# Composing units of the last pass taken into the expert blocks, and first coefficients ahead of units

## The reference, cut to what matters

```python
h = h + _L0_attn_ref(_layernorm(h), ...)   # a state-space scan, 16 states, 256 channels
h = h + _L0_ffn_ref(_layernorm(h), ...)    # top 2 of 8 experts, each 256 -> 1024 -> 256, gated
h = h + _L1_attn_ref(_layernorm(h), ...)   # a gated recurrence
h = h + _L1_ffn_ref(_layernorm(h), ...)    # W1, W2 composed: see below
...

def _compose_weight(logits, A, B):
    vals, idx = jax.lax.top_k(logits, TOP_K)          # 32 of 64
    w = jax.nn.softmax(vals / TEMPERATURE)
    return jnp.einsum('k,kir,kro->io', w, A[idx], B[idx])
W1 = _compose_weight(fc1_logits, fc1_A, fc1_B)        # 256 x 1024
W2 = _compose_weight(fc2_logits, fc2_A, fc2_B)        # 1024 x 256
```

## Time and profile before

| what | value |
|---|---|
| time, median of 3 | 1849.72 us (1848.54 to 1851.34) |
| profiled execution | 1853.17 us, span 1851.4 us |
| PE, DVE, ACT, POOL busy | 91%, 43%, 27%, 23% |
| granted TensorE clock, mean | 0.929 |
| DMA | 129.17 MB, mean 70 GB/s |

### The profile page before, as it was taken

How to read it: one execution, slowest core, us unless ns; L and a number is a source line. 1 busy time by engine, 2 the same in 40 slices (tenths; PEclk the granted TensorE clock), 3 DMA queues, 4 the chain that set the end, 5 groups by cost and what they waited for, 6 DMA issues and landing times.

```text
span 1851.4 us, 22690 instructions
## 1 busy us (share of the span) xinstructions
PE 1680.1 (91%) x8028; PEld 1167.6 (63%) x8028; DVE 798.7 (43%) x1698; ACT 498.6 (27%) x962; POOL 418.0 (23%) x430
## 2 busy tenths in 40 slices
PE   5877499988999999999949999999899989998999
PEld 4532134437999999999935555776864456667444
DVE  3531499987111111111126760122456555675455
ACT  1234344541212221212116323123110035543000
POOL 0363577771111111211121000000100012232000
PEclk8989799997899999999989979999579999998999
DMA  5233434434344344404161000010000010000000
GB/s 168 66 94 95 110 106 96 101 71 150 146 160 175 150 160 159 162 28 160 33 182 39 1 1 28 1 46 1 1 1 0 1 46 1 1 1 1 12 17 20
DMA packets 59046, 129.17 MB, mean 70 GB/s; under 512 B 10563, under 2 KB 39268, under 8 KB 52388
## 3 DMA queue, kind: packets, MB, share of 16 engines
q1 hardware_dynamic: 54996, 116.96, 19.8%
q0 software_dynamic: 3936, 10.75, 1.7%
HBM read 196.35 MB, written 9.97 MB: 111 GB/s over the span
## 4 chain that ended last, share of the span: by engine, by line
PE 75%; DVE 10%; SPq 5%; issue 4%; POOL 3%; ACT 2%; DMA 1%; DVEq 0%; ACTq 0%; POOLq 0%
PE psum L727 39%; PE psum L1030 13%; PE psum L759 7%; PE psum L822 4%; SPq L627 3%; DVE work L1734 3%; PE psum L737 2%; PE psum L1009 2%; PE psum L938 2%; DVE work L1868 1%; SPq L624 1%; DVE work L1867 1%; POOL xn L1937 1%; ACT work L1130 1%; PE psum L1039 1%
## 5 line engine op out<-in xcount | busy, mean ns | idle before, releaser
L727 PE MATMUL psum<-work 128*128 128x128 f32 (+3 forms) x3400 | 470.4, 300 | 16.1 <-DMA work<-in_xp 15.9
L727 PEld LDWEIGHTS psum<-work 128*128 128x128 f32 x3400 | 440.0, 193 | 33.5 <-DMA work<-in_xp 15.9
L1030 PE MATMUL psum<-w_late,xn 128*128 128x512 f32 x544 | 242.0, 603 | 0.0
L1801 DVE TENSOR_TENSOR work<-sq,psum 128x512 f32<-128x512 f32 x82 | 56.3, 687 | 387.3 <-PE psum L727 387.3
L1030 PEld LDWEIGHTS psum<-w_late,xn 128*128 128x128 f32 x544 | 103.5, 193 | 128.6 <-issue 119.2
L822 PE MATMUL psum<-work,xn 128*128 128x408 f32 (+1 forms) x320 | 152.9, 591 | 31.9 <-POOL work L1959 31.4
L1734 DVE TENSOR_TENSOR_SCAN work<-psum,work 128x414 f32<-128x414 f32 (+1 forms) x160 | 158.8, 1058 | 43.2 <-POOL work L1959 38.9
L1959 POOL TENSOR_TENSOR work<-work 128x408 f32<-128x408 f32 (+1 forms) x160 | 160.9, 1039 | 58.0 <-PE psum L822 29.6
L1918 POOL TENSOR_TENSOR rs<-rs,power 128x4 f32<-128x4 f32 (+3 forms) x40 | 44.6, 1115 | 547.2 <-DVE rs L1428 540.9
L1618 DVE SCALAR_TENSOR_TENSOR h<-psum,gate,h 128x256 f32<-128x256 f32 x272 | 119.4, 480 | 106.8 <-PE psum L1030 104.1
L1130 ACT ACTIVATE work<-psum 68x364 f32<-68x364 f32 (+10 forms) x256 | 108.0, 463 | 139.5 <-PE psum L727 57.5
(11 more groups left out here) (266 smaller groups left out, 2052.9 us busy)
## 6 DMA issues: line engine op xcount, KB each, us to landing
work<-in_W SPq DMA_DIRECT2D x123, 1024.0 KB
work<-c_rows SPq DMA_DIRECT2D x48, 204.0 KB, 3.1
w_attn<-in_B SPq DMA_DIRECT2D x64, 128.0 KB, 2.4
work<-c_rows SPq DMA_DIRECT2D x32, 238.0 KB, 3.2
w_attn<-in_A SPq DMA_DIRECT2D x64, 64.0 KB, 2.2
w_attn<-in_A SPq DMA_DIRECT2D x32, 128.0 KB, 2.5
work<-in_A SPq DMA_DIRECT2D x32, 128.0 KB, 2.5
work<-y_rows SPq DMA_DIRECT2D x8, 512.0 KB, 7.8
```

What stands on the lines that cost most here:

```text
L727: mm = pe.matmul(dst, lhs(k), rhs(k), start=(k == 0), stop=(k == parts - 1))
L1030: mm = pe.matmul(dst.rearrange("p (e n) -> p e n", e=2), xn[:, k, i * P:(i + 1) * P], w_last[:, 2 * q:2 * q + 2, k, :], start=(k == 0), st ...
L1801: dve.tensor_tensor(hm[:, j % 2, 4 * q:4 * q + 4, :].rearrange("p k n -> p (k n)"), sa[:, i % 2], A.at(("e3", j, q)), ALU.mult).then_inc(s ...
```

## The change

The last pass gets 16 places of its own: eleven over `xtok` and five over `xn`, which no expert block uses. SP issues one of its units in each of the blocks 4 to 19, behind that block's weight loads, and once waits that the x rows are stored out of `xtok`. ScalarE scales one in each of the blocks 24 to 39. All sixteen report on one semaphore, waited for as a whole. The gathered y go to `ytok`, over `w13` and the start of `w2`, since `xtok` is taken. PE's order is unchanged. In the scan, the rows of steps 0 to 3 are loaded first, and units 32 to 37 follow the rows of steps 4 to 9, one each.

```diff
@@ places
-        late_slots = [work[:, (1 - r // 5) * 2 * HALVES * HIDDEN + r % 5 * (PHALF + D):][:, 0:PHALF + D] for r in range(LATE_SLOTS)]
...
+        ytok = work[:, 0:SLOTS * TILES * D].rearrange("p (s i n) -> p s i n", s=SLOTS, i=TILES)
+        xtok_flat = xtok.rearrange("p s i n -> p (s i n)")
+        xn_flat = xn[:].rearrange("p k t -> p (k t)")
+        late_slots = [xtok_flat[:, r * (PHALF + D):(r + 1) * (PHALF + D)] for r in range(XTOK_SLOTS)]
+        late_slots += [xn_flat[:, r * (PHALF + D):(r + 1) * (PHALF + D)] for r in range(PAIRS - XTOK_SLOTS)]
...
+            return sem("slot0"), 64 * (BRIDGE // PSLOTS + PAIRS)
@@ SP, load_unit
-                if i >= BRIDGE:
-                    if i in (BRIDGE, BRIDGE + 5):
-                        sp.wait_ge(sem("e3_done"), 2 * (BLOCKS if i > BRIDGE else BLOCKS - 1))
-                    if i >= BRIDGE + LATE_SLOTS:
-                        sp.wait_ge(sem("tile_used"), i - LATE_SLOTS + 1)
-                elif i >= PSLOTS:
+                if PSLOTS <= i < BRIDGE:
                     sp.wait_ge(sem("tile_used"), i - PSLOTS + 1)
@@ SP, scan
-            for i in range(PSLOTS):
-                load_unit(EARLY + i)
             for k in range(CHUNKS * N_STATE):
                 load_c(k)
+                if CRING <= k < CRING + PSLOTS:
+                    load_unit(EARLY + k - CRING)
@@ SP, blocks
+                if j == 3:
+                    sp.wait_ge(sem("x_stored"), 16 * len(GROUPS))
+                if 4 <= j < 4 + PAIRS:
+                    load_unit(BRIDGE + j - 4)
-            for i in range(BRIDGE, BRIDGE + LATE_SLOTS):
-                load_unit(i)
...
-                    sp.dma_start(xtok[:, k, t0:t1, :], y_rows[k * TOKENS:(k + 1) * TOKENS].rearrange(
+                    sp.dma_start(ytok[:, k, t0:t1, :], y_rows[k * TOKENS:(k + 1) * TOKENS].rearrange(
...
-            for i in range(BRIDGE + LATE_SLOTS, PASSES * PAIRS):
-                load_unit(i)
@@ ScalarE
-            for i in range(5):
-                scale_unit(BRIDGE + i)
+                if 8 + PAIRS <= j < 8 + 2 * PAIRS:
+                    scale_unit(BRIDGE + j - 8 - PAIRS)
             keep_y(BLOCKS - 1)
-            for i in range(5, LATE_SLOTS):
-                scale_unit(BRIDGE + i)
...
-            left = list(range(BRIDGE + LATE_SLOTS, PASSES * PAIRS))
             for d in range(DUOS):
-                if d < len(left):
-                    scale_unit(left[d])
                 ln(L1A, [d])
```

More of the change, by code:

```diff
@@ L52 @@
 BRIDGE = 3 * PAIRS
-LATE_SLOTS = 10
+XTOK_SLOTS = 11
 RING = 3
@@ L268, in build, with unit_loaded @@
         in_block = work[:, at0[0]:at0[0] + SLOTS * TILES * 2 * BLOCKS].rearrange("p (i a j) -> p i a j", a=2, j=BLOCKS)
+        ytok = work[:, 0:SLOTS * TILES * D].rearrange("p (s i n) -> p s i n", s=SLOTS, i=TILES)
[3 more added lines that the diff above has]
+        late_slots += [xn_flat[:, r * (PHALF + D):(r + 1) * (PHALF + D)] for r in range(PAIRS - XTOK_SLOTS)]
+        unit_long = lambda i: tile_long[i % PSLOTS] if i < BRIDGE else late_slots[i - BRIDGE][:, 0:PHALF]
+        unit_short = lambda i: tile_short[i % PSLOTS] if i < BRIDGE else late_slots[i - BRIDGE][:, PHALF:]
+        def unit_loaded(i):
+            if i < BRIDGE:
+                return sem(f"slot{i % PSLOTS}"), 64 * (i // PSLOTS + 1)
+            return sem("slot0"), 64 * (BRIDGE // PSLOTS + PAIRS)
         xblk = take(XR * D).rearrange("p (r n) -> p r n", r=XR)
@@ L1806, in _ @@
                 dve.wait_ge(sem("y_summed"), d + 1)
-                dve.tensor_tensor(flat(h, d), flat(h, d), flat(xtok[:, 0], d), ALU.add).then_inc(h_ready, 1)
+                dve.tensor_tensor(flat(h, d), flat(h, d), flat(ytok[:, 0], d), ALU.add).then_inc(h_ready, 1)
                 stats(L1A, d)
@@ L1988, in sum_y @@
                 pool.wait_ge(sem(f"gathered{d // 2}"), 16 * SLOTS)
-                pool.tensor_tensor(flat(xtok[:, 0], d), flat(xtok[:, 0], d), flat(xtok[:, 1], d), ALU.add).then_inc(
+                pool.tensor_tensor(flat(ytok[:, 0], d), flat(ytok[:, 0], d), flat(ytok[:, 1], d), ALU.add).then_inc(
                     sem("y_summed"), 1)
```

## The result

The changed kernel takes 1818.5 us (1817.7 to 1819.0), the kernel before beside it 1850.5; the ratio is 0.982 (95% interval 0.980 to 0.984). That is 32 us less, forecast were 34.2 (1815.5), with a range of 1808 to 1824; the time is 3.0 us above the forecast and inside the range. The profiled executions differ by 34.2 us in their span (1851.4 and 1817.2). The total is near, but its two terms are not: the tail (from the end of the last expert block to layer 1) gave 26.7 us where 24.0 were forecast, and the scan 5.8, seen at the first expert block, where 10.2 were.

The account below looks back on a forecast made before the run. After the last expert block, SP's pace of writing DMAs was taken to bound the kernel; second came the scan's start. Tail 24.0 plus scan 10.2 gave 34.2 us, from 1849.7 to 1815.5; range 1808 to 1824.

Parts of the forecast that it names:

- (a): Start of the tail: last y's scatter lands 4.4 us after issue, so the gather starts 21.3 us earlier, at 933.1.
- (b): Tail, gather to next stage: VectorE's 26 us moves 21.3 us earlier as a block; PE's last transposes end at 970.7.
- (c): Tail's end: ScalarE, no longer late by scales, lets PE start in1 at 972.5, not 996.5; tail gain 24.0 us.
- (d): Expert blocks: the moved loads and scales of 16 units cost 0, with 0 to +3 us.
- Rival D: Expert blocks: units ahead of the next expert's weights in SP's queue stall blocks; 1875 at 3.75 us each; chance 0.04.
- E: Expert blocks: the units' landing waits or the moved scales hold ScalarE; 1839.5 at worst; chance 0.04.
- C: Tail: scatter lands late, or PE at half clock sets the end; gain 18 instead of 24, 1821.5; chance 0.14.
- B: Scan: the new order gives nothing, step 10 ends where it did; 1826; chance 0.06.
- part 2: Scan: coefficients ahead of units start GpSimd 16.6 us earlier, SP's pace takes back 6.4; gain 10.2 us.
- Rival A: Scan: the new order keeps its whole gain of 16.6 us; 1809; chance 0.10.

Follow-up runs that it names:

- units ahead of the weights: The changed kernel with each unit of the last pass asked for ahead of its block's w13 load on SP; 1815.7 us, ratio 0.982.
- late scales: The changed kernel with the last pass's unit loads still early, but their 16 scales back in ScalarE's old places; 1815.4 us, ratio 0.982.
- part 1 alone: The changed kernel with the scan's old order, units 32 to 37 ahead of the first coefficients; 1823.7 us, ratio 0.986.
- part 2 alone: The kernel before with only the scan's new order of coefficients and units 32 to 37, tail as before; 1844.4 us, ratio 0.9975.

## Why the prediction was right, and where it was not

**The tail's start, (a).** The mechanism is as forecast, the size of one term was not. The scatter was taken to land 4.4 us after its issue; SP's first gather DMA is at 925.63, 2.46 us after 923.17, below even the low end of the earlier trace rows, 2.6, where its median, 4.4, was taken. From the last block to the gather it is 3.32 us, forecast 5.0, before 26.3: 1.7 us of the miss. By the 2.0 us and bytes over 436 GB/s of the Trainium skill (DMA: Bandwidth & Descriptors, Anatomy of one DMA) an estimate for this scatter of 128 KB is 2.3 us. With 2.46 us the trace agrees, and the long delay that the same section warns of for writes to HBM did not show.

**From the gather to in1, (b) and (c).** Forecast 39.4 us, measured 925.63 to 964.03, 38.4. The first sum came 5.62 us after the first gather DMA (6.04 before); this gave 0.4 us. VectorE's block is the same to 0.02 us. From its last normalising (956.96) to in1's second product it was 7.07 us, forecast 7.65: the other 0.6. Most of this is the step from ScalarE's last copy to TensorE, for which the sum had 0.4 us (972.1 to 972.5) and the trace has 0.04. The pause of TensorE was 1.5 us, not 3, which changed nothing in the sum. So the tail gives 68.4 - 41.7 = 26.7 us, not 24.0.

**The blocks, (d).** Free, as said: 443.29 against 443.28 us from the first block to the join. The run with units ahead of the weights shows that the slack is real, and how large in the tightest block: 4.2 us of delay of each w13 load bring one wait, of 0.20 us. Rival D, which needed 2.1 us in each of 16 blocks, is out; with the late scales, E is too. C is out by the landing and by the clock, which was at its full 2.4 GHz level (granted 1.00) from 940 to 952 us; B by step 10.

**The scan.** The mechanism is as forecast: SP's writing takes back a part of the gain. Mis-sized were the price per step and the landing, and the sum passed the whole gain at step 10 on to the first block. SP was taken at 4.15 us for a row and a unit: it is 4.38 to 4.79, 4.48 in the mean (SP's timeline: rows at 197.58, 201.96, 206.36, 210.75, 215.18 and 219.97). A row written right behind a unit takes 0.58 us of SP where one by itself takes 0.32, in the kernel before too (203.92 and 210.2); the prediction had 0.40 for it. Landing and start on GpSimd was 4.16 us for row 10 (219.97 to 224.13), not 3.9. So step 10 ended at 226.3, not 224.6: 8.5 us gained and not 10.2. The waits began at step 7, with 1.82 us; the prediction's working holds GpSimd from step 7 on, its list of signs names only steps 8, 9 and 10.

Of these 8.5, 5.8 arrived at the first block in this profile. From the end of step 10 to the first block the kernel before took 250.0 us and the changed one 252.7. TensorE's first four groups of out0 alone took 15.0 and 17.5 us of it, by the granted clock: 2.5 of the 2.7. This stretch has the same products in all these kernels, and its length follows the execution: 250.0, 251.2 and 250.8 us with the old order (before twice, part 1 alone), 252.7, 250.7, 250.5, 246.5 and 246.2 with the new one (changed kernel twice, units ahead of the weights, part 2 alone, late scales). In the two of 246 us the four groups took 12.7 and 12.8 us. So a single profile can't say whether part 2 gives 5 or 10 us.

Two figures stand for what part 2 gives. By the marks of these eight profiles the first block starts at 484.4 us in the mean with the old order and at 475.7 with the new one, 8.7 us earlier, as much as at step 10. By the times of part 2 alone, twelve against seventeen, it is 4.8 us (interval 2.6 to 6.7), which is the better figure for the time, since the profile of part 2 alone is of the fastest of the twelve (1839.8, median 1844.4). Why that is less than the 8.5 at step 10 stays open.

**The sum.** The profiled spans differ by 34.2 us: 5.8 at the first block, 26.7 in the tail, and the last 1.7 behind out1's start, where the clock fell one group later in the changed kernel. The same stretch, last pieces of out1, in the kernel before (granted 0.50 from 1091.5 to 1112) and in the changed one (1.00 at 1059, 0.51 from 1060.8 to 1078):

```profile
1091.47 2.06 PE L759 MATMUL psum<-w_attn,work 128*128 128x256 f32 x4 [2.25 <-DVE work L1829]
```
```profile
1059.03 1.13 PE L754 MATMUL psum<-w_attn,work 128*128 128x256 f32 x4 [2.25 <-DVE work L1819]
```

The next piece starts 3.14 us behind this one before and 1.69 us behind it in the changed kernel, 1.45 of the 1.7.

That the span's difference equals the forecast to the tenth is luck: two terms were off by 2.7 and -4.4, and the clock gave 1.7. The time, 1818.5, is inside the range by the same luck, since the two misses have opposite signs. Rival A (the whole stall of the scan saved) was wrong for this change; with the units spread the stall is saved whole at step 10. That this kernel takes 1809, the figure A had, is in part luck too, since A's sum has 24 us for the tail.

## What to carry to other kernels

A queue that issues DMAs has a pace of its own: here 0.47 us a DMA and 0.4 us an index load (0.27 and 0.15 in two steps), which with the short steps between them makes 3.8 us for a unit. Count a queue's instructions between two that someone waits for, and compare with the step of the engine that waits; then place bulk loads as far apart as their deadlines allow, not in the first steps that are free. Where the work of a pass has no input from the tokens, a long stretch bound by one engine is the place for its loads, and it cost nothing in 16 blocks. Before a term of the size of the run-to-run spread is explained, compare marks inside two profiles of the same kernel.

## What the runs showed of the hardware that I had not expected

The granted TensorE clock falls at the chunk ends of the scan in some executions and not in others of the same kernel. The products of out0 of chunk 1, behind the same pause of 2.69 us, took 3.72, 5.41, 6.62 and 6.63 us in two profiles each of the two kernels. The stretch from step 10 to the first block spreads over 246.2 to 252.7 us, for the most part by this. The scatter of the last y, 128 KB to HBM, let SP go on 2.46 us after its issue. A row of coefficients landed 3.3 to 4.1 us after its issue beside one unit per step, and the two rows written from 212.39 on in the run with a unit every second step took 5.8 and 6.6. And the weight loads of 2 MB have room here: asked for 4.2 us later, they made TensorE wait 0.20 us in one block.
